# Causal attention: the future masked by VectorE in place of mask products on TensorE

## What is computed

```python
q = (x @ Wq.T + bq).reshape(B, T, H, D)          # T = 2048, H = 16, D = 8
k = (x @ Wk.T + bk).reshape(B, T, H, D)
v = (x @ Wv.T + bv).reshape(B, T, H, D)
q, k = apply_rope(q, sin, cos), apply_rope(k, sin, cos)
scores = jnp.einsum('bqhd,bkhd->bhqk', q, k) / math.sqrt(D)
scores = jnp.where(causal[None, None], scores, -jnp.inf)
probs = jax.nn.softmax(scores, axis=-1)
out = jnp.einsum('bhqk,bkhd->bqhd', probs, v).reshape(B, T, C)
```

## Time and profile before

| | us |
|---|---|
| median of three runs | 4052.3 |
| lowest, highest | 4043.87, 4054.38 |
| the profiled execution, its own time | 4049.78 |
| its span, first to last instruction | 4047.9 |
| the causal stage in it, first product to last turn | about 2586.7 to 3086 |

### The profile page before, as it was taken

One profiled execution on the slowest core, in us unless ns is written; L12 is line 12 of the kernel. 1 busy time (PEld: TensorE's weight loads), 2 busy tenths in 40 slices (PEclk: granted clock), 3 DMA queues, 4 the chain that ended last, 5 costly groups with the idle time before them and its releaser, 6 DMA issues.

```text
span 4047.9 us, 71976 instructions
## 1 busy us (share of the span) xinstructions
PE 3594.8 (89%) x29276; PEld 1462.3 (36%) x29276; DVE 3088.4 (76%) x6440; ACT 2272.1 (56%) x2630; POOL 138.7 (3%) x371
## 2 busy tenths in 40 slices
PE   5889889779999996799999987599997899999886
PEld 3755756412222223122222263233333122222362
DVE  5255545589999955899999547796875899999547
ACT  2222232228888882388888821157475388888821
POOL 0000000110000000000000000200000000000000
PEclk8889889869999997699999989699998699999988
DMA  0010510120000002200000000400001200000000
GB/s 29 2 50 1 119 38 1 35 86 2 2 2 2 2 2 57 86 2 2 2 2 2 23 1 0 115 2 2 2 2 41 75 2 2 2 2 2 23 1 11
DMA packets 32731, 84.57 MB, mean 21 GB/s; under 512 B 10096, under 2 KB 25232, under 8 KB 26000
## 3 DMA queue, kind: packets, MB, share of 16 engines
q1 hardware_dynamic: 32256, 78.17, 7.2%
q10 hardware_dynamic: 144, 1.79, 0.1%
HBM read 65.24 MB, written 14.70 MB: 20 GB/s over the span
## 4 chain that ended last, share of the span: by engine, by line
DVE 46%; PE 45%; ACT 4%; issue 3%; DMA 2%; SPq 1%; POOL 0%; ACTq 0%; DVEq 0%; POOLq 0%
DVE pm L1874 37%; PE ps L1815 9%; PE ps L1780 6%; PE ps L1800 4%; PE ps L949 3%; PE ps L952 3%; PE ps L2099 3%; PE ps L2075 3%; PE ps L1028 3%; ACT arena L1840 1%; PE ps L1477 1%; PE ps L1212 1%; PE ps L748 1%; DVE XN L293 1%; DVE stat L283 1%
## 5 line engine op out<-in xcount | busy, mean ns | idle before, releaser
L1874 DVE TENSOR_REDUCE pm<-ps 128x1 f32<-128x512 f32 (+2 forms) x3712 | 2214.5, 668 | 140.4 <-PE ps L1780 75.7
L1840 ACT ACTIVATE arena<-ps 128x1024 f32<-128x1024 f32 (+3 forms) x1856 | 1851.8, 1001 | 510.8 <-PE ps L1800 357.9
L1780 PE MATMUL ps<-arena 64*128 64x512 bf16 (+2 forms) x3712 | 1298.5, 396 | 29.1 <-DVE pm L1874 15.4
L1815 PE MATMUL ps<-arena,VA 128*16 128x256 f32 (+1 forms) x14592 | 1138.5, 384 | 40.4 <-ACT EV L1860 22.9
L1800 PE MATMUL ps<-arena 64*128 64x512 bf16 (+1 forms) x3712 | 1043.7, 379 | 21.5 <-DMA arena<-m_dram 20.7
L1780 PEld LDWEIGHTS ps<-arena 64*128 64x128 bf16 x3712 | 330.5, 93 | 1081.6 <-DVE pm L1874 894.9
L1815 PEld LDWEIGHTS ps<-arena,VA 128*16 128x16 f32 x14592 | 240.5, 94 | 511.0 <-ACT arena L1840 404.0
L1800 PEld LDWEIGHTS ps<-arena 64*128 64x128 bf16 x3712 | 195.7, 94 | 122.8 <-issue 78.6
L968 ACT ACTIVATE EV<-ps 128x512 f32<-128x512 f32 x128 | 76.3, 597 | 203.0 <-PE ps L949 203.0
L980 DVE TENSOR_TENSOR arena<-EV,ps 128x512 f32<-128x512 f32 x128 | 87.9, 687 | 124.8 <-PE ps L952 120.3
L949 PE MATMUL ps<-XNT,arena 128*128 128x512 f32 x304 | 160.7, 611 | 2.3 <-DVE arena L1255 1.5
(11 more groups left out here) (270 smaller groups left out, 2680.3 us busy)
## 6 DMA issues: line engine op xcount, KB each, us to landing
arena<-parts_dram SPq DMA_DIRECT2D x192, 128.0 KB, 2.9
parts_dram<-parts SPq DMA_DIRECT2D x32, 384.0 KB, 2.9
arena<-k_dram SPq DMA_DIRECT2D x20, 528.0 KB, 11.4
arena<-in_pad SPq DMA_DIRECT2D x16, 512.0 KB, 8.0
parts<-k_dram SPq DMA_DIRECT2D x8, 528.0 KB, 6.6
arena<-in_w SPq DMA_DIRECT2D x4, 1024.0 KB, 6.2
early<-in_late SPq DMA_DIRECT2D x1, 2184.5 KB, 8.9
VA<-k_dram SPq DMA_DIRECT2D x4, 528.0 KB, 7.7
```

Of the source, the lines that this page charges most:

```text
L1780: ins = e.matmul(bank[:, 0:w], QR[half(par), q, 2 * g + pp, qt * P:(qt + 1) * P], KT[half(par), kc, 2 * g + pp, 0:w], start=True, stop=not ...
L1815: ins = e.matmul(c.bank(4)[32 * hh:32 * hh + VW, a:b], c.VA[:, j, GH * g + hh, :], self.PB[:, (first + hh) % self.PBS, a:b], start=j == 0 ...
L1840: e.activation(self.PB[:, s:s + 2, offs[0]:CH], c.bank(t % 4, 2).rearrange("p (a t) -> p a t", a=2)[:, :, offs[0]:CH], ACT.Exp, scale=self ...
L1874: e.tensor_reduce(c.pm[:, u % 2, at, kc:kc + 1], self.slot_bank(slot)[:, 0:w], AX, ALU.max).then_inc(self.emptied_v.sem, 1)
```

## The change

Both kinds of mask product are gone from TensorE. For the maxima, VectorE's reduction over a diagonal slot becomes one instruction that adds a row of 512 values, zeros followed by the triangle (`future`), to the bank, writes the sum to SBUF (`masked`, three places in `XN`) and gives the maximum of it (`tensor_tensor_reduce`). GpSimd builds `future` at the stage's start, in the space of the first parts, once those are stored, and VectorE waits for it before its first maximum. For the turned scores a new step "cut" stands between "scores" and "exp" of a diagonal pair: VectorE adds the triangle to 128 columns of both banks in place, and the exponential waits for this in place of the product. In the order of steps nothing else moves.

```diff
--- before.py
+++ after.py
@@ -1579,7 +1579,7 @@
         self.causal = causal
         self.units = [(g, NC - 1 - k if g % 2 else k) for g in range(NG) for k in range(NC)]
         self.steps, self.slots, self.tiles, self.exps = [], 0, 0, 0
-        self.later = []
+        self.later, self.cuts, self.cut_of = [], 0, {}
         self.exp_of, self.tile_off, self.turned = [], [], []
         self.rows_slot, self.out_slot, self.last_max, self.last_tile = {}, {}, {}, {}
         self.lay_out()
@@ -1626,7 +1626,12 @@
         first = self.tiles
         self.tiles += 2
         self.tile_off += [off, off]
-        self.steps += [("scores", u, j, pp, first), ("exp", first, 2, self.exps)]
+        self.steps.append(("scores", u, j, pp, first))
+        if self.causal and j >= TPC * q:
+            self.steps.append(("cut", first))
+            self.cut_of[first] = self.cuts
+            self.cuts += 1
+        self.steps.append(("exp", first, 2, self.exps))
         self.exp_of += [self.exps] * 2
         self.exps += 1
 
@@ -1695,6 +1700,10 @@
         self.PB = chip.arena[:, 16384:16384 + self.PBS * CH].rearrange("p (n t) -> p n t", n=self.PBS)
         self.zeroed = sig.claim("value_bank_zeroed", 1)
         self.prepared, self.gathered = before, before.gathered
+        if causal:
+            self.future = chip.f32_parts[:, 0:CH]
+            self.masked = chip.XN[:, :, :].rearrange("p (s i) n -> p s (i n)", s=NC)
+            self.future_set = sig.claim("future_masked", 2)
         self.filled = sig.claim("slot_filled", p.slots)
         self.emptied_v = sig.claim("slot_emptied_vector", p.slots - n)
         self.emptied_s = sig.claim("slot_emptied_scalar", n)
@@ -1704,6 +1713,7 @@
         self.m_in = [sig.dma(f"maxima_rows{k}", n) for k in range(2)]
         self.scored = sig.claim("scores_made", p.tiles // 2)
         self.exped = sig.claim("scores_exped", p.exps)
+        self.cut = sig.claim("future_cut", p.cuts)
         self.valued = sig.claim("values_added", p.tiles // 4)
         self.copied = sig.claim("context_copied", n)
         self.inverse = sig.claim("sums_inverted", n)
@@ -1718,6 +1728,11 @@
     def gpsimd(self, e):
         c = self.c
         s = self.split
+        if self.causal:
+            for stored in self.prepared.stored[0:2]:
+                e.wait_ge(*stored[1])
+            e.memset(self.future[:, 0:CH - P], 0.0).then_inc(self.future_set.sem, 1)
+            e.tensor_copy(self.future[:, CH - P:CH], c.MQB[:, :]).then_inc(self.future_set.sem, 1)
         for u in range(len(self.plan.units)):
             k = u % 2
             e.wait_ge(*self.top[u])
@@ -1775,12 +1790,9 @@
                     e.wait_ge(*self.gathered[chunk][-1])
                 n_chunks = max(n_chunks, q + 1, kc + 1)
                 bank = self.slot_bank(slot)
-                diag = self.causal and kc == q
-                w = (qt + 1) * P if diag else CH
+                w = (qt + 1) * P if self.causal and kc == q else CH
                 ins = e.matmul(bank[:, 0:w], QR[half(par), q, 2 * g + pp, qt * P:(qt + 1) * P],
-                               KT[half(par), kc, 2 * g + pp, 0:w], start=True, stop=not diag)
-                if diag:
-                    ins = e.matmul(bank[:, w - P:w], c.IDB[:, :], c.MQB[:, :], start=False, stop=True)
+                               KT[half(par), kc, 2 * g + pp, 0:w], start=True, stop=True)
                 ins.then_inc(self.filled.sem, 1)
             elif what == "rows":
                 _, u, slot = step
@@ -1791,18 +1803,13 @@
                 _, u, j, pp, t = step
                 g, q = plan.units[u]
                 off = plan.tile_off[t]
-                diag = self.causal and j >= TPC * q
                 if j == 0 and pp == 0:
                     e.wait_ge(*self.m_in[u % 2][u + 1 - (u % 2)])
                 if t > 3:
                     e.wait_ge(*self.exped[plan.exp_of[t - 4]])
                 for par in range(2):
                     ins = e.matmul(c.bank((t + par) % 4)[:, off:CH], KT[half(par), j // TPC, 2 * g + pp, j % TPC * P:(j % TPC + 1) * P],
-                                   QR[half(par), q, 2 * g + pp, off:CH], start=True, stop=not diag)
-                if diag:
-                    for par in range(2):
-                        ins = e.matmul(c.bank((t + par) % 4)[:, off:off + P], c.IDB[:, :], c.MKB[:, :], start=False,
-                                       stop=True)
+                                   QR[half(par), q, 2 * g + pp, off:CH], start=True, stop=True)
                 ins.then_inc(self.scored.sem, 1)
             elif what == "values":
                 _, u, j, first, last, part = step
@@ -1833,7 +1840,7 @@
             if step[0] == "exp":
                 _, t, n, x = step
                 offs, s = plan.tile_off[t:t + n], t % self.PBS
-                e.wait_ge(*self.scored[(t + n - 1) // 2])
+                e.wait_ge(*(self.cut[plan.cut_of[t]] if t in plan.cut_of else self.scored[(t + n - 1) // 2]))
                 if t + n > self.PBS:
                     e.wait_ge(*self.valued[(t + n - 1 - self.PBS) // 4])
                 if n == 2 and offs[0] == offs[1]:
@@ -1863,16 +1870,27 @@
         c, plan = self.c, self.plan
         e.wait_ge(*self.prepared.mid[-2])
         e.memset(c.bank(4), 0.0).then_inc(self.zeroed.sem, 1)
+        if self.causal:
+            e.wait_ge(*self.future_set[-1])
         for step in plan.steps:
             what = step[0]
             if what == "max":
                 _, u, pp, qt, kc, par, slot = step
                 g, q = plan.units[u]
-                w = (qt + 1) * P if self.causal and kc == q else CH
                 at = (2 * pp + par) * TPC + qt
+                top, bank = c.pm[:, u % 2, at, kc:kc + 1], self.slot_bank(slot)
                 e.wait_ge(*self.filled[slot])
-                e.tensor_reduce(c.pm[:, u % 2, at, kc:kc + 1], self.slot_bank(slot)[:, 0:w], AX,
-                                ALU.max).then_inc(self.emptied_v.sem, 1)
+                if self.causal and kc == q:
+                    w = (qt + 1) * P
+                    e.tensor_tensor_reduce(self.masked[:, slot % 3, 0:w], bank[:, 0:w], self.future[:, CH - w:CH], 1.0, NEG, ALU.add,
+                                           ALU.max, top).then_inc(self.emptied_v.sem, 1)
+                else:
+                    e.tensor_reduce(top, bank, AX, ALU.max).then_inc(self.emptied_v.sem, 1)
+            elif what == "cut":
+                t = step[1]
+                block = c.bank(t % 4, 2).rearrange("p (a t) -> p a t", a=2)[:, :, plan.tile_off[t]:plan.tile_off[t] + P]
+                e.wait_ge(*self.scored[t // 2])
+                e.tensor_tensor(block, block, bc(c.MKB[:, :], 2), ALU.add).then_inc(self.cut.sem, 1)
             elif what == "finish":
                 u = step[1]
                 g, q = plan.units[u]
```

## The result

The changed kernel takes 4029.5 us (median of five runs, 4025.2 to 4032.0) against 4052.3 (4043.9 to 4059.0) of the kernel before: a ratio of 0.9947 with a 95% interval of 0.9934 to 0.996; by the ratio it is 21.5 us faster (16 to 27). A second comparison on another chip gave 0.9948 [0.9931, 0.9964].

The account below looks back on a forecast made before the run. The prediction took VectorE to bound the causal stage's first kind of stretch and TensorE the second. VectorE's added work outweighed TensorE's gains by +15.0 us, giving 4067 in median terms against 4052.3, range 4042 to 4096.

Parts of the forecast that it names:

- In the first, VectorE is the bound: First of two kinds of causal-stage stretch, VectorE taken as full: 13.27 us busy of 14.21 in unit 1's diagonal.
- TensorE's gain here is worth nothing, as VectorE ends last: Diagonals of units 1 to 3, coming twice: only VectorE's added work was counted, +14.2 us.
- classes 1 and 2: Diagonals of units 1 to 3 and 9 to 11, +14.2 us, and the stretches between them, +6.3 us.
- cheap rival: Cut at 0.29, free accumulator, 0.1 us more from each removed mask of some 100 maxima: -15 us, 4037; chance 0.09.
- Classes 2 and 3: VectorE-full stretches between diagonals, without cuts, +6.3 us; unit 7, whose steps carry 32 maxima, +4.9 us.
- class 2: VectorE-full stretches between diagonals, without cuts: 8 + 10 + 12 diagonal maxima at 0.1 us, twice: +6.3 us.
- class 6: TensorE-paced diagonals of units 4, 5, 6, 12 and 13: -1.2 us each, -6 us in all.
- floor of 8.65: Diagonals of units 4 to 6: unit 14's bare latency chain, 7.65 us, plus 1.0, against 10.23 and 10.45.
- extra hop: Latency chain of diagonals: the masks' 0.22 us becomes a VectorE wait, 0.42 and a hop, +0.25 us per two steps.
- The start of the stage: First maximum waits for GpSimd's triangle: some 2 us of delay under 13 us of cover, costing nothing.
- The rival that the masks were on nobody's path: Neither masks nor cuts on the critical path: a small sum within 12 us of nothing, 4052; chance 0.17.
- the dear side: Accumulator read at 0.19 adds 11 us, 4078; clock falls give 4085 to 4098; chance beyond 4080 is 0.16.

Follow-up runs that it names:

- run 2: Changed kernel with the turned scores' mask products put back on TensorE, only the diagonal maxima masked by VectorE: 4023.9 us, ratio 0.9931 to before.
- run 4: Kernel before with a spare 256-element VectorE addition, SBUF to SBUF, at the place of every cut: ratio 1.0035, +14 us.
- run 8: Kernel before with the mask product of every diagonal maximum issued twice: ratio 1.0004, +2 us.
- hybrid: Changed kernel with cuts on VectorE only in units 4, 5, 12 and 13, pairs of mask products elsewhere: 4015.1 us, ratio 0.9922 to before.
- run 9: Kernel before, unchanged, measured and traced once more: 4058.9 us.
- run 3: Changed kernel with both masks left out, so its result is not the attention's: 4002.6 us, ratio 0.9877 to before.
- run 7: The hybrid with the mask products of the maxima of units 1 and 9 back on TensorE: 4022.8 us, ratio 0.9933 to before.
- run 10: The hybrid with every product of the maxima of units 8 and 9 issued twice: 4019.1 us, ratio 0.991 to before.

## Why the prediction was wrong

**What bounds the kernel: the failed step.** "In the first, VectorE is the bound" holds for units 1 and 7 in part (unit 1's chain gives VectorE 45.7%) and not for units 2 and 3. I read busy time as occupancy. The busy time of a VectorE row is the union of shown durations, and each carries about 0.08 us in which the next instruction may already have started. I knew this of TensorE ("ends are modelled") and priced its masks by starts, but took VectorE by shown durations. Unit 3's 8.99 busy of 11.94 was already only 75%. With it stood "TensorE's gain here is worth nothing, as VectorE ends last": run 2, which takes masks from TensorE and gives VectorE almost nothing, shortens the stretches of classes 1 and 2 by 12.8 us. I made unit 3's stretch longer all the same, by adding 3.4 and 0.6 and dividing by 0.96, which gives 13.5 us from a load of 13.0: an engine that is busy 75% can't be full. Even by shown durations the sum was 1.1 us over the 11.94, and by starts (10.7) it is 1.2 under. In run 4 eight additions disappear in each of units 2 and 3, and the chain of waits in unit 3 of before gives VectorE 5.4%.

**The price of the cut.** 0.42 us, shown 0.428 and held 0.335: 128 x 0.085 = 11 us too much. The end of 0.29 that I gave to the cheap rival was nearer.

**The accumulator.** 0.1 us each; a read is shown as 83 ns and costs 0.01 by starts, so 26 us are 3. The nearest row, ScalarE's read of 194 ns, was of another engine, and half of it was no better than nothing. The Trainium skill (VectorE: DVE Perf Modes, "Two Vector instructions with no wait between them") is right that there are two instructions: 256 reads stand in the groups. Its second instruction was not a second price here. Classes 2 and 3 contain the difference: class 2 was forecast as accumulator alone, 6.3 us, and came out as +0.3, with gains of 0.2 to 1.0 us in four of six stretches and losses of 1.4 and 1.7 ahead of unit 1's and 9's diagonals, which ran at clocks of 0.86 and 0.81.

**The gain of a mask on TensorE.** The slots of 0.17 and 0.22 us were right for what a mask product holds (run 8 has 0.16 again). What they leave out is that a mask also keeps the products around it apart, and that this ends with the mask: 0.31 us for the pair in place of 0.22, and a product for the maxima that begins with a score product and not 0.38 us ahead of it. I had set this aside with the argument that a drain would lie inside the measured slot. So class 6 gave -10.9 for -6, with units 4 and 5 at 7.7 and 7.8 us, below the floor of 8.65 that I had built from the bare chain. The extra hop was over-priced too: unit 14's diagonal takes 8.03 where it took 7.61 from exponential to exponential (the 7.65 of the earlier trace rows starts 0.04 us early), so a cut costs the chain 0.10 per two steps and not 0.25. Even 8.03 is no floor for units 4 and 5, which lie below it; why they do is open.

**Unit 0, 7 and 8.** Unit 7's +3.5 for +4.9 is right in size for the wrong reason. The hybrid has no cuts there and takes 21.78 us (run 6), and the kernel before takes 23.20 in another execution (run 9): that the forecast met the size is luck with the clock, 0.54 in the profile of after and 1.00 in the one of before. By the two profiles of each kernel, all stretches sum to 466.9 and 478.0 before and 449.0 and 447.3 after. The difference by profiles is thus 18 to 31 us, and the medians' 21.5 lies in it.

**The start of the stage** came out as forecast. The first maximum waits 1.93 us for the triangle, and the rows that hang on it go out at 2604.18, 22 us later (before, they went out at 2610.46); nothing of it is paid.

```profile
2582.40 0.29 DVE L1885 CUSTOM_DVE_ANT_0 XN<-ps,parts 128x128 f32<-128x128 f32 x1 [1.93 <-POOL parts L1735]
...
2604.18 0.58 SPq L1762 DMA_DIRECT2D m_dram<-mt  x1
```

**The rivals.** The cheap rival named all three terms that came true: the cut near 0.29, a free accumulator, and score products that run side by side once no mask parts them. It had -15 us with a chance of 0.09, and "from where VectorE's additions stay below 35 us". They are 45 us and the change still gains, since in units 2 and 3 the additions fell into room that I took for used. Its third term was too small and went to the wrong units: maxima without masks were worth 28 us alone (run 2). The rival that the masks were on nobody's path is refuted by run 3 (-50 us). Of the dear side, the accumulator did not come, and the fused maximum shows 685 ns at 512, as the plain one. The falls of the clock did: the mean granted clock is 0.915 in both profiles of after and 0.921 and 0.916 in those of before, and the time came out lower all the same. What the falls cost the change is not settled.

The range failed with the same step. It bounded the prices (0.29 to 0.68, 0 to 0.19) but not whether a stretch was VectorE's at all, and the sum of class 1 and 2, 20 us, stood on that.

**What stays open.** Why the granted clock falls to 0.5 to 0.6 near unit 7 in most executions and holds at 1.00 in some: the kernel before has shown both, run 8 held it, run 7 did not, and run 10 held it in part. With one or two profiles of each kernel, no run tells what decides it. How much of the 10 us between the hybrid and the change is the clock's is not settled either.

## What to carry to other kernels

Before an engine is called full in a stretch, count what it holds by starts: how long after each instruction the next one begins where they stand back to back. Then ask the chain of waits for that stretch; it must name the engine. Shown durations make a short instruction look up to a third dearer than it is (0.42 for 0.33 us, 0.28 for 0.21). Work moved between two engines that are both nearly full should be moved stretch by stretch: here the kernel that has cuts only in four units of sixteen has the lowest median of those that compute the mask.

## What the runs showed of the hardware

- VectorE, back to back: an instruction of 512 fp32 columns from PSUM starts 0.60 us before its follower, one of 256 over two banks 0.33, a fused one of 128 0.21; their records show 0.68, 0.42 and 0.28.
- A fused addition and maximum with an operand in PSUM and one in SBUF takes 685 ns at 512 columns, as the plain maximum. The read of its accumulator is a record of its own, 83 ns, and adds 0.01 us.
- A 128x128 mask product between products on 64 rows, or ahead of value products in column groups, holds TensorE 0.16 to 0.17 us; a second one right behind it 0.06. A score pair of 256 columns is followed by a product on 64 rows after 0.12 us and by a mask after 0.21.
- The granted clock of one stretch isn't a property of the kernel: the same kernel ran unit 7 in 18.15 us at 1.00 and in 23.20 at 0.63.
